# Conv attention: the 3x3 convolution on eight tiles of the TensorE array, without halo transfers, and column sums by folds

## The reference

```
gx = groupnorm(x) as [256, 16, 128, 128]
channel_weight = sigmoid(gn1(conv1x1([mean(gx), max(gx)])))          # one number a channel
pos_h = sigmoid(conv1x1(conv1x1(mean of gx over w)))                 # one a row and channel
pos_w = sigmoid(conv1x1(conv1x1(mean of gx over h)))                 # one a column and channel
sx = conv3x3(gx * pos_h * pos_w, 16 -> 16 channels, SAME) + b_s3
out = x + gx * channel_weight * sigmoid(gn2(sx))
```

## Time and profile before

| what | us |
|---|---|
| median of three runs | 4297.4 |
| the profiled execution, whole | 4296.2 |
| its span, first to last instruction | 4294.3 |
| TensorE busy | 4041.4 |
| VectorE busy | 4018.4 |
| ScalarE busy | 2624.4 |
| GpSimd busy | 1775.4 |

### The profile page before, as it was taken

The page is one execution under the profiler, slowest core; times in us unless marked ns, Lnnn a source line. Parts: engine busy times, 40 slices in busy tenths (PEclk is TensorE's granted clock), DMA queues, the critical chain, the costliest instruction groups (busy, mean ns, idle before and its releaser), DMA issues.

```text
span 4294.3 us, 55492 instructions
## 1 busy us (share of the span) xinstructions
PE 4041.4 (94%) x11016; PEld 1938.2 (45%) x11016; DVE 4018.4 (94%) x2719; ACT 2624.4 (61%) x4354; POOL 1775.4 (41%) x2314
## 2 busy tenths in 40 slices
PE   5999999999999999999999999999999999999997
PEld 2444444444444444444444444444444444444443
DVE  7999999999999999999999999999999999999996
ACT  3566566666665666666656666666666666665665
POOL 3443444444434434443344434344444344434443
PEclk9999999999999999999999999999999999999998
DMA  6777777777777777777777777777777777777775
GB/s 124 163 173 173 172 175 169 175 172 173 172 173 169 177 173 172 175 167 178 172 172 172 172 176 172 171 172 176 168 177 173 172 175 167 177 173 173 171 177 123
DMA packets 1147751, 730.57 MB, mean 170 GB/s; under 512 B 74144, under 2 KB 1122976, under 8 KB 1147552
## 3 DMA queue, kind: packets, MB, share of 16 engines
q1 hardware_dynamic: 1147552, 728.87, 74.7%
HBM read 268.64 MB, written 268.44 MB: 125 GB/s over the span
## 4 chain that ended last, share of the span: by engine, by line
DVE 53%; issue 18%; SPq 11%; DMA 9%; PE 6%; POOL 1%; ACT 1%; DVEq 1%; POOLq 0%; ACTq 0%
DVE sums L560 13%; DVE mx L607 12%; SPq L222 11%; DMA xt<-in_x 9%; DVE sp_buf L524 7%; DVE sums L554 7%; DVE gated L567 7%; DVE sp_buf L527 6%; PE conv_ps L637 5%; POOL rstd L275 1%; ACT sp_buf L416 1%; DVE gate_hr L594 0%; PE pos_ps L637 0%; DVE ch L603 0%; DVE sums_n L545 0%
## 5 line engine op out<-in xcount | busy, mean ns | idle before, releaser
L637 PE MATMUL conv_ps<-gated,W_conv 128*128 128x512 f32 x6144 | 2973.1, 619 | 16.5 <-DVE gated L567 16.3
L637 PEld LDWEIGHTS conv_ps<-gated,W_conv 128*128 128x128 f32 x6144 | 1143.4, 197 | 1100.0 <-issue 1071.7
L637 PE MATMUL conv_ps<-halo,W_halo 96*128 96x512 f32 x2048 | 1027.7, 604 | 2.1 <-DMA halo<-gated 1.6
L370 ACT ACTIVATE sp_buf<-conv_ps,weights 128x1024 f32<-128x1024 f32 x512 | 565.3, 1104 | 747.8 <-PE conv_ps L637 747.5
L323 POOL TENSOR_TENSOR gated<-gate_w,gate_hr 128x2048 f32<-128x2048 f32 x256 | 918.7, 3609 | 166.9 <-DVE gate_hr L594 157.6
L560 DVE TENSOR_REDUCE sums<-xt 128x128 f32<-128x2048 f32 x256 | 943.6, 3725 | 0.0
L554 DVE TENSOR_REDUCE sums<-xt 128x16 f32<-128x2048 f32 x256 | 584.2, 2282 | 171.5 <-DMA xt<-in_x 171.4
L524 DVE SCALAR_TENSOR_TENSOR sp_buf<-xt,negm,sp_buf 128x2048 f32<-128x2048 f32 x256 | 600.6, 2346 | 38.3 <-ACT sp_buf L416 38.3
L527 DVE SCALAR_TENSOR_TENSOR sp_buf<-sp_buf,kfac,xt 128x2048 f32<-128x2048 f32 x256 | 602.1, 2352 | 9.0
L567 DVE SCALAR_TENSOR_TENSOR gated<-xt,negm,gated 128x2048 f32<-128x2048 f32 x256 | 593.9, 2361 | 0.0
L343 POOL TENSOR_TENSOR rstd<-var_e,consts 128x2 f32<-128x2 f32 x128 | 89.8, 701 | 1176.8 <-DVE var_e L581 1176.8
(11 more groups left out here) (79 smaller groups left out, 2174.4 us busy)
## 6 DMA issues: line engine op xcount, KB each, us to landing
xt<-in_x SPq DMA_DIRECT2D x2048, 128.0 KB, 3.0
out<-sp_buf SPq DMA_DIRECT2D x2048, 128.0 KB, 2.5
halo<-gated SPq DMA_DIRECT2D x512, 365.2 KB, 6.0
weights<-in_by_channel SPq DMA_DIRECT2D x1, 116.5 KB, 2.6
S_chan<-in_same_channel SPq DMA_DIRECT2D x1, 64.0 KB, 1.9
whalo_in<-in_wconv SPq DMA_DIRECT2D x2, 3.0 KB, 1.8
masks<-in_row_masks SPq DMA_DIRECT2D x1, 12.0 KB, 1.9
hmask<-in_halo_mask SPq DMA_DIRECT2D x1, 3.0 KB, 1.9
```

The costliest lines, as they stand in the source:

```text
L370: nc.scalar.activation(sp_buf[:, g, k * 8:k * 8 + 8], conv_ps[:, h % 2], ACT.Identity, bias=V["b_s3"], accum_out=ssum2[:, g, k:k + 1]).the ...
L637: return nc.tensor.matmul(ps, lhsT, rhs, start=start, stop=stop)
```

## The change

- Partitions are ordered by row pairs: partition 32 (r // 2) + 2 c + r % 2. Output rows 2o and 2o + 1 of all 16 channels are then 32 neighbouring partitions.
- Row r of a block needs rows r - 1 to r + 1. For output pair o, input rows of the upper 64 partitions (r = 0 to 3) and of the lower 64 (r = 4 to 7) are read separately, as tiles of 64 rows and 32 columns of the array. Where a row lies in the neighbouring block, the tile reads its 4 blocks one block further up or down: the lower half for pair 0 and the upper half for pair 3. `gated` gets an empty block at either end. The masks wrap around (modulo 8). There is no halo, no W_halo and no halo DMA.
- Per kernel column, bank and half there are four small matmuls in place of one large: 192 a unit in place of 32. The upper half of bank n alternates with the lower half of bank n - 1, so that they write different banks; the lower half of the last bank of a unit comes in slot 0 of the next. PSUM holds four banks, evacuated one at a time.
- Column sums: fold8 adds blocks 0 to 7 and 8 to 15, fold4 halves that again, and four matmuls with W_cols sum the rest, inside `positions`. sums_n goes: the mean enters by matmuls of negm with unscaled weights (W_rows_m, W_cols_m).
- The order of TensorE's and ScalarE's small work changes with it.

```diff
-                        nc.vector.tensor_reduce(sums[:, dc, j, NB:], xt[:, sc, j].rearrange("p b w -> p w b"), AX_X,
-                                                ALU.add).then_inc(sums_done, 1)
+                        n = 2 * c + j
+                        if later(n, 1):
+                            dve.wait_ge(fold4_done, n)
+                        nc.vector.tensor_tensor(fold8[:], xt[:, sc, j, 0:8], xt[:, sc, j, 8:16],
+                                                ALU.add).then_inc(fold8_done, 1)
+                        dve.wait_ge(fold8_done, n + 1)
...
+                        nc.vector.tensor_tensor(fold4[:, dc, j], fold8[:, 0:4], fold8[:, 4:8],
+                                                ALU.add).then_inc(fold4_done, 1)
...
-                        mm(pos[:, :, 0:NB], W_rows[:, :], sums_n[:, da, :, 0:NB])
-                        mm(pos[:, :, NB:NB + W], W_cols[:, :], sums_n[:, da, :, NB:]).then_inc(pos_mm, 1)
+                        shift = negm[:, sa].unsqueeze(2)
+                        mm(pos[:, :, 0:NB], W_rows[:, :], sums[:, da], stop=False)
+                        mm(pos[:, :, 0:NB], W_rows_m[:, :], shift.to_broadcast([P, 2, NB]), start=False)
+                        for i in range(4):
+                            mm(pos[:, :, NB:NB + W], W_cols[:, :], fold4[:, da, :, i], start=i == 0, stop=False)
+                        mm(pos[:, :, NB:NB + W], W_cols_m[:, :], shift.to_broadcast([P, 2, W]),
+                           start=False).then_inc(pos_mm, 1)
...
+                def tiles(u, d, n, half, kw, start):
+
+                    j, k = n // BANKS, n % BANKS
+                    for o in range(PAIRS):
+                        band = 1 + BB * k
+                        if half == 1 and o == 0:
+                            band -= 1
+                        if half == 0 and o == PAIRS - 1:
+                            band += 1
+                        rows = slice(ROW_TILE * half, ROW_TILE * (half + 1))
+                        cols = slice(QUAD * o, QUAD * (o + 1))
+                        ins = mm(conv_ps[cols, k], W_conv[rows, kw, cols],
+                                 gated[rows, d, j, band:band + BB, kw:kw + W], start=start and kw == 0,
+                                 stop=not start and kw == KW - 1)
+                    return ins
+
+                def slot(n, first=0, last=KW):
...
+                    for kw in range(first, last):
+                        if real(t):
+                            ins = tiles(t, q % 2, n, 0, kw, True)
...
+                        if real(t) if n > 0 else real(b):
+                            if kw == 0:
+                                pe.wait_ge(upper_mm, 8 * t + n)
+                                pe.sem_inc(upper_ready, 1)
+                            if n > 0:
+                                ins = tiles(t, q % 2, n - 1, 1, kw, False)
+                            else:
+                                ins = tiles(b, sb_ % 2, 7, 1, kw, False)
+                            if kw == KW - 1:
+                                ins.then_inc(conv_mm, 1)
...
+                slot(0)
+                slot(1)
                 mean2(b, sb_, 1)
+                positions()
+                slot(2)
+                slot(3, 0, 1)
                 variance()
+                channel()
+                slot(3, 1, KW)
+                slot(4)
                 var2(b, sb_, 1)
+                slot(5)
                 mean2(t, q, 0)
+                slot(6)
+                slot(7)
                 var2(t, q, 0)
```

More of the change, by code:

```diff
@@ L73, in conv_attention @@
         S_chan = sb("S_chan", [P, P])
-        sums = sb("sums", [P, 2, 2, NB + W])
-        sums_n = sb("sums_n", [P, 2, 2, NB + W])
+        sums = sb("sums", [P, 2, 2, NB])
+        fold8 = sb("fold8", [P, 8, W])
+        fold4 = sb("fold4", [P, 2, 2, 4, W])
+        W_rows_m = sb("W_rows_m", [P, P])
+        W_cols_m = sb("W_cols_m", [P, P])
         tot = sb("tot", [P, 2, 2])
@@ L457, in body @@
                 if real(t):
[L458 removed]
+                    evacuate(t, q, 3)
                 if real(b):
@@ L536, in body @@
                     finish(b, sb_, 0)
-                if real(a):
-                    dve.wait_ge(negm_done, a + 1)
-                    if later(a, 2):
-                        dve.wait_ge(pos_mm, a - 1)
-                    for j in range(2):
-                        nc.vector.tensor_scalar(sums_n[:, da, j, 0:NB], sums[:, da, j, 0:NB], 1.0 / W,
-                                                negm[:, sa, j:j + 1], ALU.mult, ALU.add)
-                        ins = nc.vector.tensor_scalar(sums_n[:, da, j, NB:], sums[:, da, j, NB:], 1.0 / NB,
-                                                      negm[:, sa, j:j + 1], ALU.mult, ALU.add)
-                    ins.then_inc(sn_done, 1)
                 def row_sums(j):
@@ L693, in channel @@
                         mm(cw_ps[:, 0:2], W_gmp[:, :], gmx_n[:, da], start=False).then_inc(ch_mm, 1)
-                def conv(h, first, last):
-                    if not real(t):
-                        return
-                    j, k = h // 2, h % 2
-                    d = q % 2
-                    if first == 0:
-                        pe.wait_ge(mod_done, 2 * t + j + 1)
-                        if later(4 * t + h, 2):
-                            pe.wait_ge(evac, 4 * t + h - 1)
-                    for i in range(first, last):
-                        w, bank = i // 2, i % 2
-                        band = (2 * k + bank) * BB
-                        o = conv_ps[:, h % 2, bank * BB:(bank + 1) * BB]
-                        if w < KW:
-                            mm(o, W_conv[:, w], gated[:, d, j, band:band + BB, w:w + W],
-                               start=w == 0, stop=False)
-                        else:
-                            if bank == 0:
-                                pe.wait_ge(halo_in[d][j], 16 * (t - d) + 32)
-                            rows = halo[:, d, j].rearrange("p (b w) -> p b w", w=WP)
-                            ins = mm(o, W_halo[:, :], rows[:, band:band + BB, 0:W], start=False)
-                    if last == 8:
-                        ins.then_inc(conv_mm, 1)
```

188 lines of the change are left out of this document (85 added, 103 removed).

## The result

The changed kernel takes 5641.27 us (median of 4 runs, 5639.81 to 5642.82), the kernel before 4296.56: a ratio of 1.3128 [1.3106, 1.3151], so it is slower by 1345 us, 10.5 us for each of 128 units. The direction is the forecast's, the time lies in its range, and the size is short by 640 us.

A forecast was written before the change was run, and what follows sets the result against it. Bound: VectorE's order of work, closed over the load of x. 27.5 + 3.2 + 5.3 + 2.0 = 38.0 us a unit against 32.57, +680 us and 20 at the start: 5000 us; own range 4750 to 5350, overall 3900 to 6300.

The forecast's parts named there:

- Tiles side by side: TensorE's convolution: eight tiles run at once, so 192 small matmuls are 24 rounds of 0.86 us, 20.6 us a unit.
- tiles in turn: Rival, TensorE: upper and lower half run in turn, 46 us a unit, 6020 us in all; chance 0.07.
- held back: Rival, TensorE: a tile's second pass waits for its first and holds back the next tile; 11,200 us; chance 0.10.
- Column sums: VectorE: four folds take 3.9 us a unit in place of two reductions, saving 3.5 us.
- The folds pass first: VectorE and GpSimd after gate_hr: folds run before the gate products; the channel norm then falls under two modulates and two finishes.
- The sigmoid stall: VectorE's finish of the next unit waits 5.3 us for the gate's sigmoid, behind the delayed channel norm.
- Products about 4 us after gate_hr: GpSimd's products begin then and end at 11.3 to 11.5 us; VectorE's maxima_in waits for the second, stalling 3.2 us.
- var_e and gates: VectorE waits for var_e 1.1 us behind late evacuation and TensorE work, gates 0 to 2.5; taken as 2.0 together.
- Sum: One unit: 27.5 us of VectorE work plus stalls of 3.2, 5.3 and 2.0 make 38.0 us, against 32.57.
- collision in the folds: Rival: products come right after the first fold and alternate with the folds; 35.6 us a unit, about 4680 us; chance 0.10.
- faster: Rival: exclusion between VectorE and GpSimd costs little; both TensorE and VectorE near 29.2 us a unit, about 3870 us; chance 0.22.

The follow-up runs named there:

- norm_last_ch: norm_last with TensorE's two channel matmuls issued behind slot 5 instead of between slot 3's first and second third; 4297.34 us.
- products_first: The changed kernel with GpSimd issuing the two gate products before the power of unit t-1's second group instead of behind it; 4782.31 us.
- folds_only: The kernel before with only column sums by two folds and four accumulated matmuls, and no sums_n; convolution, halos and partition order left; 4628.93 us.
- reorder_pos: norm_last_ch with VectorE reordered (var_e before finish, maxima beside products, folds between modulates), positions behind slot 3's first third and variance, var2 before slot 4; 3940.45 us.
- norm_last: The changed kernel with GpSimd's channel_norm behind the first group's power, the channel gate's sigmoid in the next unit, kfac behind channel_in; 4553.77 us.
- filler: The changed kernel with six more matmuls on TensorE in each unit, into unused columns just ahead of unit t-1's mean2; 5532.35 us.

## Why the prediction was right in kind and short in size

- **Tiles side by side, 20.6 us for 24 rounds.** Right: a slot is 2.81 us where the forecast had 2.6, with all eight tiles at work; the rivals with tiles in turn or held back fall. The rule of the Trainium skill (TensorE: Matmul & The Clock Gate, part 3 on packing), that matmuls on different tiles start and end strictly in program order, did not bring the case that I derived from it: two passes of one tile in a row do not hold up the next tile, as 48 passes in 2.81 us show. The records don't say which tile a pass is for, so the rule itself is not tested here, only my case.
- **Column sums 3.9 us.** Right: 2822.34 to 2826.27.
- **The folds pass first, the products come after, the norm falls into modulate and finish.** Right, in nearly every unit: over the run the folds last 1.25 and 0.72 us in the mean, the norm's first four steps 2.15 to 2.27. The sigmoid stall, put at 5.3, measures 5.36. One detail was wrong: maxima_in was to wait for the end of the second product; it waits for the first, and the modulate for the second.
- **Products about 4 us after gate_hr, a stall of 3.2.** Mis-sized: 6.6. The chain from gmx_n to var2 (TensorE: 2820.80 to 2827.65) ran with the clock at 0.73: 80 passes in 6.39 us, where slot 3's rest and slot 4 were put at 4.3 (at the upper level they take 4.9, in norm_last_ch). The stall behind the products is therefore 5.1 us (1.8 + 3.3).
- **var_e and gates 2.0.** The other mis-sized step, in this unit the larger: 5.25 (4.92 + 0.33). Its parts were right as a chain (evacuation, mean2, positions, slot 2, variance), but durations were taken from the kernel before, at the clock's upper level. From the sigmoid to var_e it was put at 8.1 us and takes 11.9 (2807.28 to 2819.22); positions alone was put at 2.6 and takes 5.4. The forecast did say that TensorE would stand idle and that this was "rather more than less", and gave that no price.
- **Sum.** 38.0 + 1.9 + 3.3 = 43.2, the 43.3 measured in this unit. Over the run the two steps are about equally short: var_e and gates come to 4.6 us a unit (546.2 and 47.9 us over 128), maxima_in and the modulates to 5.9 (1.8 and 3.2 inside them, 0.9 idle ahead of them), so 2.6 and 2.7 us more than forecast. From the first var_e to the last a unit takes 43.4 us, before 33.0: the unit of the earlier trace rows, 32.57, is 0.4 us shorter than the mean, which by luck hid some 50 us of the miss. The missing 10.4 - 5.4 = 5.0 us over 126 units are 630 us, of 641.
- **The rival "collision in the folds", 4680.** It did not come in the changed kernel, but products_first (4782) and folds_only (4629), which are other kernels, show its mechanism, near its price.
- **The rival "faster", 3870.** It needed an order in which GpSimd's norm does not decide, and the changed kernel doesn't have it. reorder_pos (3940), another kernel, comes near its limits, with VectorE 90% and TensorE 94% busy.

What the runs show and what is argued: that the seam and the place of the power carry the loss is shown by norm_last and products_first. Their gains, 1088 and 859 us, can't be added, since together they are more than the loss: each opens the same chain at another place. How the loss splits between stall and clock is not shown: filler bought only 109 us, but mended only some units.

## What to carry to other kernels

An instruction's worth is also what runs beside it. A reduction with one SBUF input was cover for GpSimd; its cheaper replacement with two inputs is none (a fold of 0.69 us held for 3.98). So price both the work saved and the cover lost, and put the cover back by order. When a chain is lengthened on TensorE, price what follows its idle time at the lower clock level. And after a large change re-time the order: here four moves were worth 1344 us, and the first three of them, with var_e ahead of a finish, gave the kernel without the change nothing.

## What the runs showed of the hardware

- Eight tiles of 64 rows and 32 columns, fp32, two passes a matmul: 48 passes of 512 columns in 2.81 us at a granted clock of 1.00, 9% over the 2.58 us of six passes of 0.43.
- TensorE, idle for 7.75 us, did the work behind it at a granted 0.50; behind an idle time of 1.61 us the mean over the next 6.3 us was 0.73.
- Most of GpSimd's small instructions (128x2, 0.20 us alone) last 2.2 to 2.3 us beside VectorE's instructions with two SBUF inputs (2.35 us), one for each; a product of 3.6 us holds such an instruction of 0.69 us for 3.98.
- Two products of GpSimd back to back let one VectorE instruction in between: maxima_in, issued at 2830.70, was done at 2832.66, and the modulate behind it had to wait out the second product.
- Six otherwise useless matmuls in TensorE's idle time made the program 109 us faster.
